# Transposed inputs loaded instead of transposed on TensorE, one buffer for two normalized contexts, and a new order table, in a four-layer cross-attention kernel

## Time and profile before

| What | Value |
|---|---|
| Median of 3 runs | 4441.46 us (4438.94 to 4445.67) |
| Profiled execution, its own time | 4448.31 us |
| Its span, first to last instruction | 4446.5 us |
| Mean granted clock of TensorE | 0.990 |
| Moved by the load engines | 52.92 MB, mean 12 GB/s |
| Chain that ended last, by engine | PE 42%, DVE 40%, issue 10%, POOL 5%, ACT 2% |

### The profile page before, as it was taken

How to read it: one execution, slowest core, us unless ns; L and a number is a source line. 1 busy time by engine, 2 the same in 40 slices (tenths; PEclk the granted TensorE clock), 3 DMA queues, 4 the chain that set the end, 5 groups by cost and what they waited for, 6 DMA issues and landing times.

```text
span 4446.5 us, 116614 instructions
## 1 busy us (share of the span) xinstructions
PE 4086.8 (92%) x45024; PEld 3473.5 (78%) x45024; DVE 2928.1 (66%) x7395; ACT 2694.5 (61%) x8513; POOL 1233.9 (28%) x2247
## 2 busy tenths in 40 slices
PE   4899999999999999999999999999999999999996
PEld 3778778787787787787787887787787877877875
DVE  2576676676666666766766766766766766766664
ACT  2566666656656656656656666666666666566563
POOL 0232322322322322323323323323223223223221
PEclk8999999999999999999999999999999999999998
DMA  3000000000000000000000000000000000000000
GB/s 122 1 11 7 11 11 6 11 11 7 11 11 6 11 11 6 11 11 7 11 9 8 11 6 11 11 6 11 11 6 11 11 6 11 11 6 11 11 3 5
DMA packets 47341, 52.92 MB, mean 12 GB/s; under 512 B 5328, under 2 KB 46288, under 8 KB 46416
## 3 DMA queue, kind: packets, MB, share of 16 engines
q1 hardware_dynamic: 46800, 45.46, 3.2%
...
## 4 chain that ended last, share of the span: by engine, by line
PE 42%; DVE 40%; issue 10%; POOL 5%; ACT 2%; DVEq 0%; DMA 0%; POOLq 0%; ACTq 0%
PE gen_ps L481 25%; PE gen_ps L473 9%; DVE negmax L957 4%; DVE masked L944 4%; POOL rstd L779 4%; DVE masked L951 4%; PE gen_ps L598 3%; DVE st L919 2%; DVE xs L929 2%; DVE zn L914 2%; ACT prob L724 2%; PE gen_ps L587 2%; PE scores_ps L556 2%; DVE negmax L946 2%; PE scores_ps L563 1%
## 5 line engine op out<-in xcount | busy, mean ns | idle before, releaser
L481 PE MATMUL gen_ps<-actT,w_sb 128*128 128x128 f32 x11264 | 1394.5, 277 | 3.4 <-ACT actT L694 3.3
L481 PEld LDWEIGHTS gen_ps<-actT,w_sb 128*128 128x128 f32 x11264 | 1325.8, 193 | 23.0 <-ACT actT L694 6.2
L724 ACT ACTIVATE prob<-scores_ps,negmax 128x128 f32<-128x128 f32 x3072 | 859.8, 406 | 330.6 <-DVE negmax L957 330.6
L779 POOL TENSOR_TENSOR rstd<-ve,consts 128x1 f32<-128x1 f32 x448 | 282.9, 631 | 1525.0 <-DVE ve L921 1000.0
L473 PE MATMUL gen_ps<-consts,prob 128*128 128x128 f32 x4096 | 591.0, 279 | 65.1 <-ACT prob L724 63.1
L694 ACT ACTIVATE probT<-gen_ps 128x512 f32<-128x512 f32 x1024 | 585.8, 638 | 59.7 <-PE gen_ps L473 59.7
L473 PEld LDWEIGHTS gen_ps<-consts,prob 128*128 128x128 f32 x4096 | 467.8, 142 | 184.9 <-ACT prob L724 147.2
L957 DVE TENSOR_REDUCE negmax<-scores_ps 128x4 f32<-128x512 f32 x768 | 492.0, 682 | 82.7 <-PE scores_ps L563 82.2
L481 PE MATMUL gen_ps<-w_sb,actT 128*128 128x256 f32 x2048 | 532.3, 383 | 2.7 <-ACT actT L694 1.9
L481 PE MATMUL gen_ps<-w_sb,wide 128*128 128x256 f32 x2048 | 467.9, 381 | 1.2 <-issue 1.2
L694 ACT ACTIVATE actT<-gen_ps 128x256 f32<-128x256 f32 (+1 forms) x576 | 276.5, 480 | 301.4 <-PE gen_ps L473 294.0
...
## 6 DMA issues: line engine op xcount, KB each, us to landing
ctx_rms<-x_dram SPq DMA_DIRECT2D x64, 128.0 KB, 2.2
ctx<-ctx_dram SPq DMA_DIRECT2D x64, 128.0 KB, 2.2
mask<-mask_dram SPq DMA_DIRECT2D x128, 64.0 KB, 2.0
out_dram<-res SPq DMA_DIRECT2D x64, 128.0 KB, 1.7
...
w_sb<-weights_dram SPq DMA_DIRECT2D x1, 2048.0 KB, 30.3
...
```

What stands on the lines that cost most here:

```text
L481: last = nc.tensor.matmul(ps, lhsT(c), rhs(c), start=(c == 0), stop=(c == chunks - 1))
L724: ins = nc.scalar.activation(prob[:, N % 4, k, :], scores_ps[:, u, k * S:(k + 1) * S], ACT.Exp, bias=negmax[:, N % 4, k:k + 1])
L779: nc.gpsimd.tensor_tensor(dst, src, const("expo")[:, 0:width], ALU.pow)\
```

## The change

Four things are changed.

1. The host passes x and the context a second time, transposed (`by_column`): for each batch 128 partitions with 2 x 128 elements, 1 KB in a row. SP loads `xT` into chunks 2 and 3 of `actT`, and `ctxT` into a new buffer. The step "xT" of PE and ACT is gone, and its DVE part is now called "rows_in". "tr" of 4 transposes x alone, and its copy is 256 wide. "keys" of 4 reads `ctxT`.
2. The host passes mask3 transposed. "mask4" is a step of DVE alone, which reads the loaded tile in SBUF and writes the factor in place.
3. `ctx_ln` is the same buffer as `ctx_rms`. POOL writes it in a step "ctx_ln" of its own, once tr2's transposes are done.
4. `LIFE` and PERIOD (67.80) are made anew.

The code, without the table:

```diff
 def bank_use(name, a, u):
-    if name in ("xT", "x2T", "h", "z", "kv2", "o2", "nT", "mask4", "down"):
+    if name in ("x2T", "h", "z", "kv2", "o2", "nT", "down"):
...
-        ctx_ln = sb("ctx_ln", [P, G, D])
+        ctxT = sb("ctxT", [P, G, C, P])
...
+        ctx_ln = ctx_rms
...
             def queries(a, b):
-                read_out(pe, f"tr{a}" if a else "xT", b)
-                end(transposed(begin(f"m{a}", b), f"qk{a}", 0, 0 if a else 2, b % G), f"m{a}", b)
+                inputs_ready(a, b)
+                src = actT[:, b % G, 0:2, :] if a else actT[:, b % G, 2:4, :]
+                end(transposed(begin(f"m{a}", b), f"qk{a}", 0, src), f"m{a}", b)
 
             def keys(a, b):
                 g = b % G
-                read_out(pe, f"tr{a}" if a else "xT", b)
+                if a == 4:
+                    pe.wait_ge(ctxT_sem(b), 16 * (b // G + 1))
+                else:
+                    inputs_ready(a, b)
+                src = ctxT[:, g, :, :] if a == 4 else actT[:, g, 2:4, :]
...
+            def inputs_ready(a, b):
+                if a:
+                    read_out(pe, f"tr{a}", b)
+                else:
+                    pe.wait_ge(xT_sem(b), 16 * (b // G + 1))
...
-                elif name == "xT":
-                    pe.wait_ge(x_in_sem(b), 16 * (b // G + 1))
-                    transposes("xT", b, halves(x_in[:, g, :]))
...
                 elif name == "tr" and a == 4:
                     read_out(pe, "o3", b)
-                    transposes("tr4", b, halves(xs[:, g, :]) + halves(ctx[:, g, :]))
-                elif name == "mask4":
-                    pe.wait_ge(mask3_sem(b), 16 * (b // G + 1))
-                    transposes("mask4", b, [mask3[:, g, :]])
+                    transposes("tr4", b, halves(xs[:, g, :]))
...
-                elif name == "xT":
-                    slot_free(act, b)
-                    copy_out("xT", b, flat(actT[:, g, 2:4, :]), D)
...
                 elif name == "tr":
-                    copy_out(f"tr{a}", b, flat(actT[:, g, :, :]), 512)
+                    width = D if a == 4 else 2 * D
+                    copy_out(f"tr{a}", b, flat(actT[:, g, :, :])[:, 0:width], width)
...
                 if name == "ctx_norms":
                     rsqrt(cve[:, g, :], crstd[:, g, :], "cve", "crstd", b, 2)
                     pool.wait_ge(sem("crstd"), b + 1)
+                    nc.gpsimd.tensor_scalar(ctx_rms[:, g, :], ctx[:, g, :], crstd[:, g, 1:2], 0.0,
+                                            ALU.mult, ALU.add).then_inc(sem("ctx_rms"), 1)
+                elif name == "ctx_ln":
+                    j, use = plan["tr2", b]
+                    pool.wait_ge(bank_full[j], use)
                     nc.gpsimd.tensor_scalar(ctx_ln[:, g, :], ctx[:, g, :], cmv[:, g, 0:1], crstd[:, g, 0:1],
                                             ALU.subtract, ALU.mult).then_inc(sem("ctx_ln"), 1)
-                    nc.gpsimd.tensor_scalar(ctx_rms[:, g, :], ctx[:, g, :], crstd[:, g, 1:2], 0.0,
-                                            ALU.mult, ALU.add).then_inc(sem("ctx_rms"), 1)
...
                 elif name == "mask4":
-                    ps = take(dve, "mask4", b)
-                    release(nc.vector.tensor_scalar(fT[:, g, :], ps[:, 0:S], 0.5, 0.5, ALU.mult, ALU.add),
-                            "mask4", b)
+                    dve.wait_ge(mask3_sem(b), 16 * (b // G + 1))
+                    nc.vector.tensor_scalar(fT[:, g, :], mask3[:, g, :], 0.5, 0.5, ALU.mult, ALU.add)\
+                        .then_inc(sem("factor4"), 1)
...
                     if b < B:
+                        sp.dma_start(actT[:, g, 2:4, :], xT_d[b]).then_inc(xT_sem(b), 16)
                         sp.dma_start(x_in[:, g, :], x_d[b]).then_inc(x_in_sem(b), 16)
                         sp.dma_start(ctx[:, g, :], ctx_d[b]).then_inc(ctx_sem(b), 16)
+                        sp.dma_start(ctxT[:, g, :, :], ctxT_d[b]).then_inc(ctxT_sem(b), 16)
                         sp.dma_start(mask1[:, g, :], mask1_d[b, 0]).then_inc(mask1_sem(b), 16)
                         sp.dma_start(mask3[:, g, :], mask3_d[b, 0]).then_inc(mask3_sem(b), 16)
```

More of the change, by code:

```diff
@@ new lines @@
+    ("queries", 0, 0, {"PE": 0.00, "DVE": 21.74}),
+    ("keys", 0, 0, {"PE": 7.24, "ACT": 16.16}),
+    ("rows_in", 0, 0, {"DVE": 12.67}),
+    ("first_row", 0, 0, {"PE": 26.11, "DVE": 32.31}),
+    ("scores", 0, 0, {"PE": 33.22}),
+    ("turn", 0, 0, {"PE": 39.63, "ACT": 50.31}),
+    ("turn", 0, 1, {"PE": 39.67, "ACT": 51.56}),
+    ("turn", 0, 2, {"PE": 41.69, "ACT": 55.04}),
+    ("soft", 0, 0, {"ACT": 42.80, "DVE": 45.81}),
+    ("soft", 0, 1, {"ACT": 44.29, "DVE": 51.02}),
+    ("soft", 0, 2, {"ACT": 44.44, "DVE": 51.34}),
@@ new lines @@
+    ("soft", 0, 3, {"ACT": 46.34, "DVE": 54.63}),
+    ("turn", 0, 3, {"PE": 49.30, "ACT": 58.40}),
+    ("values", 0, 0, {"PE": 54.72, "ACT": 62.51}),
+    ("attended", 0, 0, {"PE": 56.31, "DVE": 70.48, "POOL": 65.19}),
+    ("tr", 1, 0, {"PE": 62.45, "ACT": 79.30}),
+    ("queries", 1, 0, {"PE": 63.88, "DVE": 76.03}),
+    ("keys", 1, 0, {"PE": 66.32, "ACT": 81.82}),
+    ("stats", 0, 0, {"DVE": 70.83, "POOL": 68.19}),
+    ("norm", 0, 0, {"DVE": 71.03, "POOL": 71.03}),
+    ("first_row", 1, 0, {"PE": 74.52, "DVE": 90.60}),
@@ new lines @@
+    ("kv2", 2, 0, {"PE": 123.88, "DVE": 136.30, "POOL": 129.35}),
+    ("mean_square", 2, 0, {"DVE": 126.40, "POOL": 123.94}),
+    ("rms_norm", 2, 0, {"DVE": 128.44}),
+    ("scores", 2, 0, {"PE": 129.67}),
+    ("prob_norm", 2, 0, {"DVE": 147.42, "POOL": 140.89}),
+    ("soft", 2, 0, {"ACT": 148.72, "DVE": 141.08}),
+    ("soft", 2, 1, {"ACT": 148.99, "DVE": 141.62}),
+    ("prob_norm", 2, 1, {"DVE": 150.28, "POOL": 142.54}),
+    ("soft", 2, 2, {"ACT": 149.79, "DVE": 143.51}),
+    ("turn", 2, 0, {"PE": 143.79, "ACT": 151.39}),
@@ new lines @@
+    ("keys", 3, 0, {"PE": 186.64, "ACT": 194.71}),
+    ("scores", 3, 0, {"PE": 187.65}),
+    ("turn", 3, 0, {"PE": 192.39, "ACT": 209.19}),
+    ("turn", 3, 1, {"PE": 194.91, "ACT": 209.45}),
+    ("turn", 3, 2, {"PE": 195.55, "ACT": 209.92}),
+    ("norm_x4", 3, 0, {"DVE": 195.61}),
+    ("soft", 3, 0, {"ACT": 196.74, "DVE": 198.54}),
+    ("turn", 3, 3, {"PE": 197.45, "ACT": 211.52}),
+    ("values", 3, 0, {"PE": 197.51, "ACT": 212.13}),
+    ("attended", 3, 0, {"PE": 198.30, "DVE": 210.51}),
@@ L177 @@
+    ("soft", 4, 0, {"ACT": 237.58, "DVE": 242.54}),
+    ("values", 4, 0, {"PE": 238.38, "ACT": 243.71}),
+    ("soft", 4, 1, {"ACT": 240.37, "DVE": 243.29}),
+    ("soft", 4, 2, {"ACT": 240.42, "DVE": 243.48}),
+    ("attended", 4, 0, {"PE": 241.34, "DVE": 261.20}),
+    ("zT", 4, 0, {"PE": 242.64, "ACT": 252.31}),
+    ("soft", 4, 3, {"ACT": 243.05, "DVE": 244.50}),
+    ("o", 4, 0, {"PE": 244.36, "DVE": 264.82, "POOL": 262.81}),
+    ("norm", 4, 0, {"DVE": 265.64}),
 ]
@@ L482, in product, with transposed @@
                 return last
[L484 removed]
+            def transposed(ps, w, first, src):
                 for n in range(C):
@@ L1140, in by_row_groups, with by_column @@
     return w.reshape(-1, R, C, 2, 16).transpose(0, 2, 1, 3, 4).reshape(-1, D)
+def by_column(t):
+    return t.transpose(0, 2, 1).reshape(B, C, P, S).transpose(0, 2, 1, 3)
 def by_head(w):
```

177 lines of the change are left out of this document (66 added, 111 removed).

## The result

The changed kernel takes 4337.01 us, the median of four runs (4336.12 to 4342.83); the kernel before took 4442.45 on the same chip (4438.94 to 4445.67). The ratio is 0.9766, with an interval of 0.9749 to 0.9783: 105 us faster. It landed on rival 1's figure (4339). In the profiled execution the span is 4334.9 us and the mean granted clock 0.990, as before.

What follows compares the result with a forecast made beforehand. PE's list of work was taken as the bound, with short chains not quite covered. From 4448.3 profiled, less 42 for transposes, zero for the table, 6.85 to the median and 2 for small savings: 4397 us; own range 4365 to 4430.

Steps and rivals of the forecast that it cites:

- rival 1: The new order gains as well: waits for zn and xs go, half comes back elsewhere; 4339 us, chance 0.16.
- The removed transposes: Five transposes a batch leave PE, priced start to start at 0.66 us a batch: 42 us saved, bounds nothing to 87.
- The new table: New order of steps on all engines: gains and losses of waits cancel, zero, bounds -64 to +128 us.
- zn before zT3: PE's wait for zn ahead of zT3, after attention 3, goes: 1.2 us a batch gained.
- queries 1: After tr1, PE waits for ACT's copy without x's transposes to fill the time: about 0.4 us a batch lost.
- turn 2.0 and 2.3: PE's turns wait for POOL's normalization and a bank that queries 0 holds: about 0.5 and 0.9 us a batch lost.
- the chain to tr1: From kv2 to tr1, 6.85 us of chain over 5.9 of PE work; 1.0 uncovered, as before: about no difference.
- The bank uses: Two of 59 PSUM bank uses a batch go, easing the four-bank rotation: nothing, then 2 us with the first eviction.
- ACT, loads, shared buffer: Fewer ACT evictions, two more SyncE loads a batch and ctx_ln's wait on POOL: each costed at nothing.
- Rival 2: Chains through DVE set the pace, so the 42 us saved turn into waiting: no change, 4441 us, chance 0.12.
- Rival 3: Slower at tr1: DVE reaches kv2 late by about 1.9 us and PE idles; 4519 us, chance 0.18.
- Rival 4: DVE's mask factor, now from SBUF, collides with POOL's normalization before first_row 1: 29 us, 4426 us, chance 0.06.

Runs made afterwards that it cites:

- e12: Old table with the new paths, plus five transposes a batch on PE whose results nobody reads: 4449.02 us, 1.0016.
- e4: Changed kernel plus five transposes a batch on PE whose results nobody reads, with no eviction or bank use: 4340.13 us, 0.9768.
- e5: Changed kernel with DVE's mask factor moved behind the queries of attention 4: 4315.44 us, 0.9717.
- e6: Changed kernel with DVE's reciprocals for the first three quarters of attention 2 moved earlier: 4284.73 us, 0.9645.
- e2: Changed kernel with the old table, so new paths and shared buffer only: 4419.55 us, 0.9946.
- e1: Kernel before with the new table; x, context and mask still transposed on PE, two context buffers: 4402.52 us, 0.9921.
- e15: Changed kernel with only the mask transposed on PE again, one transpose and one bank use a batch: 4467.77 us, 1.0058.
- e16: Changed kernel with only x transposed on PE again, two transposes, one eviction and one bank use a batch: 4336.96 us, 0.976.
- e8: New table with the old paths, DVE's read of queries 0 moved ahead to free its bank for keys 0: 4356.55 us, 0.9808.
- e3: Kernel before with only ctx_ln put in ctx_rms's buffer, written by POOL in its own step: 4440.37 us, 0.9997.
- e10: Kernel before with DVE's attended 3 moved ahead of two soft steps: 4440.41 us, 0.9997.
- e13: Kernel before with the context's norms moved late on DVE and POOL: 4437.49 us, 0.9990.
- e14: Kernel before with both the context's norms late and DVE's attended 3 ahead of two soft steps: 4435.30 us, 0.9988.

## Why the prediction was right or wrong

**The bound.** "Bound by PE's list of work, with short chains that are not quite covered" holds under the old table: e12's five transposes cost 29.5 us there. Under the new one it fails in the stretch from kv2 to turn 2.3, where 320 transposes cost 3 us (e4) and moves of small DVE steps give 22 and 52 us (e5, e6).

**The sum by its terms.** The forecast was 42 (transposes) + 0 (table) + 2 (bank use, eviction) = 44 us. The runs give 22 (the paths alone, e2) + 39 (the table alone, e1) + 44 (only together) = 105. Of its signs, the 698 records a batch came (7149 / 672 x 65.63), and the large wait for zn went; a batch took 65.63 us and not 66.5 to 66.6, and PE is busy 4025.5 us and not 4045.

**The removed transposes: 42 us.** Under the old table they measured 22 (e2, taken out with all that hung on them) and 29.5 (e12, put in alone), 68 to 92 ns each: sign and order of size right, but the measured price is a third to a half below the forecast one. The missing part did not become waiting: PE's busy time itself fell by 21 us in e2 and rose by 30 in e12, with idle time 6 and 4 us less. So the distance from start to start (0.12 to 0.16 us in the prediction) overstates what a removal gives back here; why, no run shows. The Trainium skill (TensorE: Matmul & The Clock Gate, Part 4: PE-mode transpose) gives about 275 ns for one, which makes 88 us (an estimate from it). The runs don't agree with it as a price per instruction in a dense stream; the trace shows 0.27 us as the length of a lone record (mask, in e15) and 0.11 as the distance to the next start.

**The new table: "I take zero".** This is the step that failed. The items, per batch, as forecast and as the timelines of both kernels show them:

| Place | forecast | measured |
|---|---|---|
| zn before zT3 | -1.2 | -1.17 |
| first_row 1, for DVE's queries 1 | none | -0.22 |
| xs before x2T | -0.6 | -0.55 |
| scores 0, for their banks | none | -0.22 |
| a third gain in the sum, without an item | -0.4 | |
| turns of 3 and tr1 (exponentials, bank of attended 0, chain of norm 0) | 0 | 0.52 + 0.38 + 0.18 before, 0.40 + 0.68 after: 0 |
| queries 1 | +0.4 | +0.25 |
| turn 2.0 and 2.3 | +0.5 + 0.9 | +0.29 + 0.61 |
| nT | +0.5 | +0.50 |
| tr3 | +0.3 | -0.06 |

Each wait that the forecast names was found in its place, only tr3's did not grow, and the chain to tr1 balanced as forecast. The gains were put at 2.2 us and came to 2.16, two of them small ones that no item names. The losses were put at 2.6 and came to 1.59: the turns' 1.4 was 0.90, tr3's 0.3 and queries 1's 0.4 were too high as well. So the count came to 0.4 us a batch more, was called zero, and was 0.57 less (4.00 to 3.43) by the named waits and 0.78 less by PE's idle time. That is 50 us. The rest of the 60 us is busy time: 0.83 us a batch less in place of 0.66. Part of PE's busy time is the full length of the last matmul ahead of each gap. That fewer gaps leave less of it was not tried by itself.

**The bank uses: nothing, then 2 us.** The prediction costed the two uses of four banks by the ease of the rotation. Under the new table it is a partner that counts: the mask's use decides which bank keys 0 gets and is worth up to 131 us (e15), while x's is worth none (e16). The 44 us between table and paths are of this kind; that they are this bank's wholly is argued from e8 (20 us left with the wait halved) and from e15, whose wait alone makes some 54 us, and not shown to the microsecond. Under the old table the use four before keys 0 is keys 4, in the kernel before and in e2 alike, and PE has no recurring wait there.

**ACT, loads, shared buffer.** As forecast: no wait on xT but once at the start, nothing from the buffer (e3), and ACT's eviction off the path (e16).

**The rivals.** Rival 1 came true in kind: the waits for zn and xs went and about half came back elsewhere. That it fits within 2 us is luck in part: it has 58 us from the order and 42 from the transposes, where PE's idle time fell by 50 and its busy time by 61. It had 0.16 and should have had more, since the forecast's zero rested on losses that were put too high. Rival 2 (chains set the pace, so no gain) has its mechanism right in one stretch, but the waits on chains fell in all. Rival 3 fell: DVE came to kv2 on time, and tr1 waits 0.68 us. Rival 4 was real in its mechanism, and its sign (above 0.4 us) came: 413 ns on average, on the path. Beside an idle POOL the same instruction takes 217 ns (e5) and 195 in e2, less than the 262 from PSUM; so the loss is the collision and not the place of the input. e5 gives 22 us back by moving the operation, by both its shorter time and its new place. In e15 the factor is read from PSUM at the old place:

```profile
L1086 DVE TENSOR_SCALAR mask<-gen_ps x64: 260/292/293, 193.9 to 4432.0; 128x128 f32<-128x128 f32 x64
```

(shortest, median and longest ns): 292 ns against a median of 429 from SBUF. The Trainium skill's rule (SBUF — State Buffer, Who interferes with whom), that VectorE and GpSimd lock each other out for such instructions when they read SBUF, agrees with these rows: 429 ns from SBUF beside a busy POOL, 292 from PSUM beside it, 217 from SBUF beside an idle one.

**What stays open.** The table's own 39 us (e1), or 85 us with the bank freed (e8), could not be put down to a step: the two moves that the timelines pointed to gave 1 and 4 us alone and 6 together (e10, e13, e14). In e10 waits of 0.90 and 0.48 us stand where 1.17 and 0.22 stood. Whether a third move would release them was not tried.
